# Row and hidden transposes of a routed expert stage: from TensorE with PSUM copies to DMA on ScalarE's queue

## The reference

```
xf = layernorm(x)                                    # 1024 x 512
scores = sigmoid(xf @ gate_w.T + balance_bias)       # 1024 x 8
top2 -> comb[t, e] (two entries, normalised)
h = silu(einsum('td,ehd->teh', xf, w1))              # 8 experts, hidden width 1024
y = einsum('teh,edh->ted', h, w2)
out = x + einsum('te,ted->td', comb, y)
```

## Time and profile before

| | us |
|---|---|
| median of 3 runs | 619.07 |
| lowest, highest | 618.24, 622.91 |
| profiled execution, its own time | 618.08 |
| its span, first to last instruction | 616.3 |
| PE busy | 515.5 (84%) |
| DVE busy | 409.5 (66%) |
| ACT busy | 287.5 (47%) |
| POOL busy | 130.1 (21%) |
| mean granted TensorE clock | 0.925 |

### The profile page before, as it was taken

The page is one execution under the profiler, slowest core; times in us unless marked ns, Lnnn a source line. Parts: engine busy times, 40 slices in busy tenths (PEclk is TensorE's granted clock), DMA queues, the critical chain, the costliest instruction groups (busy, mean ns, idle before and its releaser), DMA issues.

```text
span 616.3 us, 11358 instructions
## 1 busy us (share of the span) xinstructions
PE 515.5 (84%) x3761; PEld 306.6 (50%) x3762; DVE 409.5 (66%) x891; ACT 287.5 (47%) x449; POOL 130.1 (21%) x100
## 2 busy tenths in 40 slices
PE   5879898889889989873840589999999999999993
PEld 2664465564557676732530245555555545455441
DVE  2837889885996969786679466766464746583430
ACT  0651657586447464755710146444542624562120
POOL 1211242340404030300175001211121121112112
PEclk9879999999999989996765679999999999999997
DMA  8991505000005996134048445777384564733222
GB/s 323 391 381 37 206 2 205 1 1 3 0 1 202 380 382 216 36 137 138 34 175 318 144 154 171 231 209 219 72 245 116 171 190 115 209 75 57 37 34 35
DMA packets 32785, 93.23 MB, mean 151 GB/s; under 512 B 2896, under 2 KB 4080, under 8 KB 28656
## 3 DMA queue, kind: packets, MB, share of 16 engines
q1 hardware_dynamic: 23984, 74.81, 34.1%
q0 software_dynamic: 4304, 9.77, 8.2%
q10 hardware_dynamic: 4464, 8.22, 4.5%
HBM read 63.36 MB, written 29.43 MB: 151 GB/s over the span
## 4 chain that ended last, share of the span: by engine, by line
PE 58%; DVE 19%; issue 11%; POOL 5%; ACT 3%; DMA 2%; SPq 0%; ACTq 0%; POOLq 0%; DVEq 0%
PE bank L680 19%; PE bank L698 18%; PE bank L340 8%; DVE small L999 5%; PE bank L505 3%; DVE ctx_region L1008 2%; POOL small L1490 2%; PE bank L539 2%; PE bank L358 2%; PE bank L598 2%; PE bank L529 2%; PE bank L422 1%; POOL routed_rows L1569 1%; DMA routed_rows<-shared,ints 1%; PE bank L452 1%
## 5 line engine op out<-in xcount | busy, mean ns | idle before, releaser
L680 PE MATMUL bank<-wbuf,ctx_region 128*128 x504 | 116.2, 388 | 6.2 <-issue 5.0
L1599 POOL DMA_INDIRECT out<-misc,ints x21 | 40.1, 1907 | 234.8 <-ACT misc L947 174.9
L680 PEld LDWEIGHTS bank<-wbuf,ctx_region 128*128 128x128 f16 x504 | 48.9, 100 | 65.7 <-issue 13.4
L1350 DVE SCALAR_TENSOR_TENSOR wbuf<-ctx_region,wbuf 128x2048 f32 (+1 forms) x28 | 62.9, 2288 | 26.0 <-ACT wbuf L865 26.0
L865 ACT ACTIVATE wbuf<-ctx_region 128x2048 f32 (+1 forms) x28 | 52.0, 1902 | 28.2 <-issue 24.3
L1490 POOL TENSOR_TENSOR small<-small 128x2 f32<-128x2 f32 (+2 forms) x25 | 25.0, 998 | 188.3 <-DVE small L1005 185.7
L954 ACT ACTIVATE ctxT_region<-bank 128x512 f32<-128x512 f32 x42 | 25.1, 597 | 76.4 <-PE bank L680 76.4
L698 PE MATMUL bank<-wbuf,actT 128*128 x264 | 58.8, 379 | 1.1 <-DVE actT L1451 1.1
L698 PE MATMUL bank<-wbuf,xn 128*128 x240 | 53.4, 379 | 0.0
L505 PE MATMUL bank<-ctx_region,wbuf 128*128 128x256 f16 x384 | 43.3, 273 | 5.2 <-DVE ctx_region L1129 3.4
L1438 DVE COPY ints<-ctx_region 128x1 int32<-128x1 int32 x22 | 3.4, 154 | 59.7 <-PE bank L340 59.7
(11 more groups left out here) (209 smaller groups left out, 896.5 us busy)
## 6 DMA issues: line engine op xcount, KB each, us to landing
ctx_region<-in_experts SPq DMA_DIRECT2D x28, 1024.0 KB, 5.3
routed_rows<-ctxT_region SPq DMA_DIRECT2D x1, 16900.0 KB, 50.6
ctx_region<-in_ctx SPq DMA_DIRECT2D x8, 1536.0 KB, 8.5
ctx_region<-routed_rows ACTq DMA_DIRECT2D x23, 260.0 KB, 2.7
wbuf<-in_experts SPq DMA_DIRECT2D x4, 1024.0 KB, 4.8
out<-x ACTq DMA_DIRECT2D x8, 256.0 KB, 2.5
x<-in_x SPq DMA_DIRECT2D x1, 1536.0 KB, 13.7
wbuf<-in_wqT SPq DMA_DIRECT2D x4, 256.0 KB, 4.6
```

The source lines that it names most:

```text
L680: mm = nc.tensor.matmul(bank[half][:, :], xgT[:, b, x_part, k * P:(k + 1) * P], w16[:, ds(at + (w_part + k * EH + half * 512), 512)], star ...
L1350: nc.vector.scalar_tensor_tensor(w16[:, ds(at + (LOW + n * PIECE), PIECE)], src_[:, piece], W_SCALE, w16[:, ds(at + (HIGH + n * PIECE), PI ...
L1599: nc.gpsimd.indirect_dma_start(out, bass.IndirectOffsetOnAxis(idx[:, slot_no:slot_no + 1].bitcast(U32), axis=0), y_out[:, slot_no, :], Non ...
```

## The change

PE no longer transposes in the expert stage. ACT issues two transposing DMA transfers per tile on its own queue: `rows_T` from `xg16[b]` (128 x 1024 f16) straight into `xgT[b]`, and `hidden_T` from `h16` (128 x 2048 f16) straight into `hT[b]`. The copies out of PSUM on DVE and ACT go. `xgT` and `hT` become semaphores that count 16 per transfer. ACT waits for the tile's `xgT` before it issues the next one, and for `h_lo` before `hidden_T`; before each issue it increments `turning`, on which nothing waits. DVE's `cut_hidden` now waits until the transfer of the tile before has landed, since `h16` is one buffer. The first product goes to banks 0 and 1 for even tiles and 2 and 3 for odd ones.

```diff
             pe.wait_ge(s["ident16"], 1)
-            def rows_T(b, landed):
-                pe.wait_ge(xg_in[b], landed)
-                transposes(bank[(4, 7)[b]][:, :].bitcast(F16), [xg16[:, b, k * P:(k + 1) * P] for k in range(2 * KC)],
-                           s["xgT_ps"], ident16)
             def experts_of(tile):
                 packed = pe.value_load(map_i[0:1, 3, ds(tile, 1)], min_val=0, max_val=16 ** 3 - 1)
...
             def first_product(tile, b, expert):
                 ready, at = expert
                 pe.wait_ge(s["w1_lo"], ready * 2)
-                pe.wait_ge(s["xgT"], tile + 1)
+                pe.wait_ge(s["xgT"], tile * 16 + 16)
                 for half in range(2):
                     for k in range(KC):
                         for x_part, w_part in ((0, HIGH), (1, HIGH), (0, LOW)):
-                            mm = nc.tensor.matmul(bank[half][:, :], xgT[:, b, x_part, k * P:(k + 1) * P],
+                            mm = nc.tensor.matmul(bank[2 * b + half][:, :], xgT[:, b, x_part, k * P:(k + 1) * P],
                                                   w16[:, ds(at + (w_part + k * EH + half * 512), 512)],
                                                   start=(k == 0 and x_part + w_part == 0), stop=(k == KC - 1 and w_part == LOW))
                     mm.then_inc(s["h_ps"], 1)
-            def hidden_T(tile):
-                for part, cut, done in ((0, s["h_hi"], s["hT_ps0"]), (1, s["h_lo"], s["hT_ps1"])):
-                    pe.wait_ge(cut, tile + 1)
-                    transposes(bank[2 + part][:, :].bitcast(F16), [h16[:, part, k * P:(k + 1) * P] for k in range(HC)], done, ident16)
             def second_product(tile, b, expert):
                 ready, at = expert
                 pe.wait_ge(s["w2_lo"], ready * 2)
-                pe.wait_ge(s["hT0"], tile + 1)
-                pe.wait_ge(s["hT1"], tile + 1)
+                pe.wait_ge(s["hT"], tile * 16 + 16)
                 for k in range(HC):
                     for h_part, w_part in ((0, HIGH), (0, LOW), (1, HIGH)):
                         mm = nc.tensor.matmul(bank[5 + b][:, :], hT[b][:, h_part, k * P:(k + 1) * P],
...
                                               start=(k == 0 and h_part + w_part == 0), stop=(k == HC - 1 and h_part == 1))
                 mm.then_inc(s["y2_ps"], 1)
-            rows_T(0, 16)
             first_product(0, 0, experts_of(0)[0])
-            rows_T(1, 16)
-            hidden_T(0)
             last = last_of(pe)
             with pe.Fori(0, (SLOT_TILES - 1) // 2) as i:
                 with pe.If(i * 2 < last):
                     experts = experts_of(i * 2)
                     for u in (1, 2):
                         first_product(i * 2 + u, u % 2, experts[u])
-                        rows_T((u + 1) % 2, i * 16 + 32)
                         second_product(i * 2 + (u - 1), (u - 1) % 2, experts[u - 1])
-                        hidden_T(i * 2 + u)
             second_product(last, 0, experts_of(last)[0])
...
                 act.wait_ge(s["y2_ps"], tile + 1)
                 nc.scalar.activation(y_out[:, b, :], bank[5 + b][:, :], ACT.Copy, scale=gates[:, b, 2:3]).then_inc(s["y2"], 1)
-            def hidden(tile, b):
+            def rows_T(b, landed):
+                act.wait_ge(xg_in[b], landed)
+                act.sem_inc(s["turning"], 1)
+                act.dma_start(xgT[:, b].rearrange("p a d -> p (a d)").rearrange("p (c t) -> p c t", t=P),
+                              xg16[:, b, 0:2 * D], transpose=True).then_inc(s["xgT"], 16)
+            def hidden_T(tile, b):
+                act.wait_ge(s["h_lo"], tile + 1)
+                act.sem_inc(s["turning"], 1)
+                act.dma_start(hT[b].rearrange("p a (c t) -> p (a c) t", t=P), h16.rearrange("p a h -> p (a h)"),
+                              transpose=True).then_inc(s["hT"], 16)
+            def hidden(tile, b, landed):
+                act.wait_ge(s["xgT"], tile * 16 + 16)
+                rows_T(1 - b, landed)
                 act.wait_ge(s["fields"], tile * 2 + 2)
                 load_rows(tile + 2, b)
                 for half in range(2):
                     act.wait_ge(s["h_ps"], tile * 2 + (half + 1))
-                    nc.scalar.activation(h[:, half * 512:half * 512 + 512], bank[half][:, :], ACT.Silu,
+                    nc.scalar.activation(h[:, half * 512:half * 512 + 512], bank[2 * b + half][:, :], ACT.Silu,
                                          scale=1.0 / W_SCALE).then_inc(s["h"], 1)
-            def hidden_copy(tile, b):
-                act.wait_ge(s["hT_ps0"], tile + 1)
-                nc.scalar.copy(hT[b][:, 0, :], bank[2][:, :].bitcast(F16)).then_inc(s["hT0"], 1)
             gate_exp(1)
             cut_high(expert0, 2 * EXPERT, (2, 3), 0)
...
             act.wait_ge(s["scattered"], 16 * 2 * TILES)
             load_rows(0, 0)
             load_rows(1, 1)
-            hidden(0, 0)
-            hidden_copy(0, 0)
+            rows_T(0, 16)
+            hidden(0, 0, 16)
+            hidden_T(0, 0)
             act.wait_ge(s["w2_lo"], 2)
             cut_high(stage, 0, (0, 1), 16 * W_PIECES)
             last = last_of(act)
             with act.Fori(0, (SLOT_TILES - 1) // 2) as i:
                 with act.If(i * 2 < last):
                     for u in (1, 2):
-                        hidden(i * 2 + u, u % 2)
+                        hidden(i * 2 + u, u % 2, i * 16 + 32)
                         cut_next_high(i * 2 + (u - 1), (2, 3))
+                        hidden_T(i * 2 + u, u % 2)
                         cut_next_high(i * 2 + u, (0, 1))
-                        hidden_copy(i * 2 + u, u % 2)
                         gated(i * 2 + (u - 1), (u - 1) % 2)
             gated(last, 0)
...
                     at = dve.value_load(map_i[0:1, 1, ds(tile, 1)], min_val=0, max_val=2 * EXPERT)
                     cut_low(stage, at * -1 + 2 * EXPERT, pieces, ready * W_PIECES)
-            def rows_copy(tile, b, again=True):
+            def rows_fields(tile, b, landed, again=True):
                 if again:
                     dve.wait_ge(s["idx"], tile - 1)
-                dve.wait_ge(s["xgT_ps"], tile + 1)
+                dve.wait_ge(xg_in[b], landed)
                 nc.vector.tensor_copy(tokens[:, b:b + 1], xg[:, b, C_TOKEN:C_TOKEN + 1].bitcast(I32)).then_inc(s["fields"], 1)
                 nc.vector.tensor_copy(fields[:, b, :], xg[:, b, C_G1:C_E2 + 1]).then_inc(s["fields"], 1)
-                nc.vector.tensor_copy(xgT[:, b].rearrange("p a d -> p (a d)"), bank[(4, 7)[b]][:, :].bitcast(F16)).then_inc(s["xgT"], 1)
-            def cut_hidden(tile):
+            def cut_hidden(tile, again=True):
                 dve.wait_ge(s["h"], tile * 2 + 2)
+                if again:
+                    dve.wait_ge(s["hT"], tile * 16)
                 nc.vector.tensor_copy(h16[:, 0, :], h).then_inc(s["h_hi"], 1)
                 dve.wait_ge(s["h_hi"], tile + 1)
                 tt(h16[:, 1, :], h, h16[:, 0, :], ALU.subtract).then_inc(s["h_lo"], 1)
-            def hidden_copy(tile, b):
-                dve.wait_ge(s["hT_ps1"], tile + 1)
-                nc.vector.tensor_copy(hT[b][:, 1, :], bank[3][:, :].bitcast(F16)).then_inc(s["hT1"], 1)
             def gate_of(tile, b):
...
                 nc.vector.tensor_copy(idx[:, b:b + 1], tokens[:, b:b + 1]).then_inc(s["idx"], 1)
             cut_low(expert0, 2 * EXPERT, (1,), 0)
-            rows_copy(0, 0, again=False)
+            rows_fields(0, 0, 16, again=False)
             cut_low(expert0, 2 * EXPERT, (2, 3), 0)
-            rows_copy(1, 1, again=False)
-            cut_hidden(0)
-            hidden_copy(0, 0)
+            rows_fields(1, 1, 16, again=False)
+            cut_hidden(0, again=False)
             cut_low(stage, 0, (0, 1), W_PIECES)
             gate_of(0, 0)
             last = last_of(dve)
             with dve.Fori(0, (SLOT_TILES - 1) // 2) as i:
                 with dve.If(i * 2 < last):
                     for u in (1, 2):
-                        rows_copy(i * 2 + (u + 1), (u + 1) % 2)
+                        rows_fields(i * 2 + (u + 1), (u + 1) % 2, i * 16 + 32)
                         cut_hidden(i * 2 + u)
                         cut_next_low(i * 2 + (u - 1), (2, 3))
                         cut_next_low(i * 2 + u, (0, 1))
-                        hidden_copy(i * 2 + u, u % 2)
                         gate_of(i * 2 + u, u % 2)
```

More of the change, by code:

```diff
@@ L79 @@
 route rt_sel rt_cnt_ps rt_exp rt_slots rt_map zrow_fill zrow xs_zero rows_set scattered
-xg_in0 xg_in1 fields xgT_ps xgT h_ps h h_hi h_lo hT_ps0 hT_ps1 hT0 hT1 y2_ps y2 gate_parts gate idx scat added out_spare
+xg_in0 xg_in1 fields xgT h_ps h h_hi h_lo hT turning y2_ps y2 gate_parts gate idx scat added out_spare
 ident16 finished staged w_hi w1_lo w2_lo""".split()
```

## The result

The changed kernel takes 650.7 us (median of 4 runs, 646.4 to 662.5) against 618.7 us before: 1.05 times as long, 95% interval 1.042 to 1.058. The forecast was 600 us, so the sign was wrong; the time lies inside the range, but far above the likeliest case's own 590 to 611.

The account below looks back on a forecast made before the run. TensorE was taken to bound the expert stage. From 618.1 us, -26.8 for transposes, +8 contention, +2, -4.3, -1.2 and +1 at the start and +0.5 at the end gave 597, rounded up to 600; range 587 to 720.

Parts of the forecast that it names:

- likeliest case: Expert stage: transposes leave TensorE and mostly hide behind products; 600 us, own range 590 to 611, chance 0.38.
- TensorE's transposes go: Expert stage's steady part: each of twenty tiles loses 1.34 us of path, -26.8 us.
- rounding: Whole sum: 597 rounded up to 600 us for ACT's in-order waits that could not be placed.
- blocks one behind another: Rival for the DMA transposes: 128x128 blocks move as if by one engine, 37 us per tile, 1120 us; chance 0.08.
- ACT's queue: ACT per tile: 4.8 us without transposes plus 2 us issue fits TensorE's 10.7; old period reached at 7.2 us issue.
- comes a product later: DVE's cut of the next tile waits for the hidden transpose's landing, but is only due a product later; no cost charged.
- ACT's queue becomes the bound: Rival on ACT's queue: long transpose issue makes TensorE wait at each second product; 690 to 780 us; chance 0.31.
- my 7.2: ACT's queue: transpose issue per tile, in us, from which ACT is longer than the old 12.0 us period.
- What a transpose costs: DMA transposes on ACT's queue: issue 1 us each, 2 per tile; hidden rows land in 5.2 us.
- the 5.0 ns of the earlier trace: Upper bound for transpose issue on ACT: dearest price per piece, from gate_w's 512 pieces; 15.5 us per tile.
- Contention (+8): Weight loads and transposes delay each other: 0.6 us on each of 13 converting tiles, +8; bounds 0 and +51.
- Start and end: Expert stage's ends: first rows +2, tile 1's product -4.3 and -1.2, tile 0's second product +1, last hidden rows +0.5.

Follow-up runs that it names:

- conversions first: Changed kernel with both pairs of ACT's weight conversions put ahead of the hidden rows' transpose: 607.7 us, 0.983 of the kernel before.
- Short conversions on ACT: Changed kernel with ACT's weight conversions in the loop cut to 64 of 2048 columns: 646.5 us.
- Silu ahead of the rows' transpose: Changed kernel loading 64 of 2048 weight columns for experts 2 to 7, Silus moved before the next tile's row transpose and the following row load: 620.8 us, 1.002.
- slivers version: Changed kernel loading only 64 of 2048 columns of each weight piece of experts 2 to 7, conversions and waits kept: 619.9 us, 1.000.
- plain copies: Both transposing transfers replaced by plain copies of the same bytes: 608.8 us (0.982) in the changed kernel, 594.1 us (0.957) with conversions first.
- two buffers: Conversions first, plus two buffers by tile parity for the cut hidden rows: 607.4 us, 0.979 of the kernel before.
- rows alone: Kernel before with only the rows transposed by DMA, hidden rows still by TensorE: 611.9 us, 0.985.
- hidden rows alone with conversions first: Kernel before with only the hidden rows transposed by DMA, both conversion pairs ahead of that transpose: 613.1 us, 0.985.

## Why the prediction was wrong, point by point

**TensorE's transposes go (-26.8).** Right. With the order put right and no weight traffic the time is 588.2 us, 30.0 under the kernel before measured beside it; the forecast's terms without contention and rounding come to -28.8. Products follow at 10.4 us a tile (548.07 and 558.43 us in that kernel's timeline). The rival of blocks one behind another is out: all sixteen blocks of the hidden rows land in 4.3 us, 0.27 us each. The Trainium skill's 1309 ns for one block by DMA (VectorE: DVE Perf Modes, section The three transpose paths) is so no price per block of a larger transfer; a single block was not run here.

**The step that failed: "ACT's queue", and the wait of DVE's cut.** I summed what stands on ACT per tile and found that it fits into TensorE's 10.7 us, and I said that DVE's cut "comes a product later". I priced a pair of conversions ahead of the transpose, at up to 1.7 us, and gave the pair behind it nothing; the runs show the reverse, since both pairs ahead is the fast order. I did not follow the one move in ACT's order that the diff shows: conversion of pieces 0 and 1 from ahead of the hidden step to behind it. There it stands behind a wait for DVE's cut and an issue of 1.4 to 7.3 us, and in front of the next tile's Silus; DVE converts later too, and its next cut is queued behind that. In the old order the conversion fills the time in which ACT waits for the cut anyway. With conversions first nearly the same work keeps up with TensorE; in the changed order the loop through both engines doesn't: in the stretch above 17.3 us against 10.7. The swap, 43 us in the whole, 30 in the hidden half and 31.7 without weight traffic, shows it. My sum for ACT also left out its register loads, 2.1 us in that stretch between the end of the issue and the conversion. Short conversions on ACT (4 us) and Silu ahead of the rows' transpose (0) shorten little of the DVE branch that the stretch shows as the longer, and bring next to nothing; how the 43 us divide between the two branches was not measured. This is the rival "ACT's queue becomes the bound", but by another mechanism than its sum of issue times: the issue was 1.26 us for the rows and 2.9 to 3.6 for the hidden ones by the medians, some 4.5 per tile, and 5.3 by the mean over all tiles of the profiled execution; both are under my 7.2. The sum was short all the same: 4.8 + 5.3 and up to 2.1 for register loads are an estimated 12.2 us, over 10.7, if nothing on ACT overlaps. With conversions first the issue runs beside the conversions, and there the work fits.

**What a transpose costs.** Forecast issue 1 us each; measured 1.26 and, without weight traffic, 1.9 to 2.2 us at the median (2.9 to 3.6 beside it). Landing of the hidden rows forecast 5.2, measured 4.3 alone, 5.6 at the median and 17.4 at worst beside weights. Of the prices per piece, the 5.0 ns of the earlier trace rows is too dear: 2048 pieces were issued in as little as 1.36 us, 0.7 ns each.

**Contention (+8).** The term was mis-sized: the weight traffic costs 19.5 us with conversions first and 31 us in the changed order. I took 21 GB/s per engine from packets of 8 KB. Those of 256 B cost more per byte. In the changed kernel (370 to 600 us)

```profile
q10 hardware_dynamic: 50702, 16.33, 46.7%
q1 hardware_dynamic: 3384, 24.58, 32.6%
q0 software_dynamic: 2160, 3.93, 11.9%
```

that is 46.7% of 16 x 230 us for 50,702 packets, 34 ns each (26 ns in the slivers version: 45.2% for 64,400), with the larger packets of the row loads counted in. At 26 ns, 3072 packets are an estimated 5.0 us of all engines per tile, not 2.3; the three queues together hold 91% of the engines. Advanced Engine Details and Errata, section X-Bar Transpose (TRN2), of the Trainium skill holds that such transposes are as fast as plain DMAs. In engine time they aren't here: the same 20.5 MB hold 43.1% of the engines with transposes and 24.5% with plain copies (conversions first in both), and with plain copies the time is 13.6 us less. How the weights' and the transposes' packets hold each other up was not resolved; smaller weight packets, tried twice, brought no gain.

**Start and end.** Rows landed to first product: 3.5 us (346.74 to 350.27) against 2.3, +1.2 where I had +2. Tile 1's product follows tile 0's without a gap, as forecast: 48 matmuls in 12.84 us. The last hidden transpose lands late:

```profile
638.03 1.97 ACTq L942 DMA_TRANSPOSE actT<-ctxT_region  x1
...
642.51 8.31 PE L685 MATMUL bank<-wbuf,actT 128*128 x24 [4.36 <-DMA actT<-ctxT_region]
```

TensorE waits 4.4 us and then runs the last product in 8.3 us against 5.4, at a mean granted clock of 0.64, so mostly at the lower level: +5 where I had +0.5.

## What to carry to other kernels

A sum of work per engine says whether a change can fit, not whether it does: when an operation moves on an in-order queue, follow what was behind it through the other engine and back, above all where the diff swaps two lines. Before a change is given up as too slow, put the old order of the neighbours back; here two lines were worth 43 us, and four versions take 1.5 to 2% less than the kernel before (conversions first 0.983, with two buffers 0.979, rows alone 0.985, hidden rows alone with conversions first 0.985). In this kernel a DMA transpose was cheap to wait for when nothing large ran beside it (4.3 us) and dear in engine time (43.1% of the engines against 24.5%): count its packets against the loads beside it.

## What the runs showed of the hardware that I had not expected

The issue of a 128 x 1024 transpose holds ACT's sequencer for 1.26 us, almost the same each time without weight traffic (1247, 1257 and 1351 ns at minimum, median and maximum), against 0.48 for a plain copy of the same bytes; beside weight loads it rises to 7.5 us. For 128 x 2048 it lies between 1.36 and 3.3 us even with no weight traffic. The landing is as steady there: 4.3 us at minimum and median. Right behind such an issue of the rows, the first load of a register by ACT takes longer. Here is the same line in the slivers version, where it follows the rows' transpose, and in the kernel before:

```profile
L914 ACTq TENSOR_LOAD <-ints x23: 303/661/707, 339.7 to 589.7; - x23
```

```profile
L930 ACTq TENSOR_LOAD <-ints x23: 273/280/486, 339.9 to 588.1; - x23
```

The median is 0.66 us against 0.28. With plain copies in the changed kernel it is 0.28 too. Behind the hidden transpose the picture is mixed: in the slivers version the median is 0.66 us, in the changed kernel 0.29.
